# Second attention of a four-layer transformer piece: a new order of the work on TensorE, VectorE and GpSimd, and a key bias added on GpSimd

## Chip, cores, metric

The kernel is one launch on one core of a Trainium2 chip. The metric is the device time of an execution in microseconds (us), as the median of several runs. A core has TensorE (PE in the rows: matmuls, and PEld, its weight loads), VectorE (DVE), ScalarE (ACT), GpSimd (POOL) and SyncE (SP, which only issues transfers here). Each runs its own instructions in the order written; semaphores tie the engines together.

## What is computed

16 sequences of 128 tokens of width 128 pass four layers, each with a residual: a cross attention on a context of 120 rows, a mixture of 8 experts with 2 picked per token, a second cross attention, and a second mixture of experts. The change is in the hand-over from the second layer to the third, and in the third:

```python
x = x + _L0_ffn_ref(_layernorm(x), ...)          # rows sorted by expert, each row of x gets two results back
xn = _layernorm(x)                               # third layer, 8 heads of 128:
q = einsum('bld,hed->bhle', xn, Wq) + bq;  k, v = the same of the context with Wk, bk and Wv, bv
attn = softmax(windowed(q @ k.T));  out = attn @ v
x = x + out.reshape(...) @ Wc.T + bc
```

The windows of the third layer count positions by head (dilations 1, 1, 2, 2, 4, 4, 8, 8), and positions past the end of the context fold onto its last row; a mask `window` of logarithms of counts, added to the scores, does both. Where a window reaches past the context's 120 rows, the key is that of the last row, so the scores need no more than the 120 columns. The key bias adds the same number to all scores of a query and head: `xn . uvec + ubias`.

## The kernel before

**Phases.** Phase a projects for the first layer, phase b is the first attention, then 46 tiles of 128 rows sorted by expert go through the experts (functions with `ct_`), then phase d is the second attention, and phase e the last layer. Every phase is a software pipeline written out by hand: each engine has a list of (lag, stage), and in step k it runs each stage on sequence k - lag, in the order of the list. The lists' order is the order of the engine's instructions, and nothing reorders them. In phase d the pipeline has 16 + 7 steps.

**Phase d, one sequence b.** PE forms the queries of all 8 heads at once from the kept, transposed activations `xT` (`d_queries`, L1716, 8 heads, 16 passes) and VectorE adds `cvec` to make `q2` (`d_queries` on VectorE, L1352). PE multiplies with the context (`d_scores`, L1725), VectorE adds the mask into `s1` (L1361, two pieces), takes the maximum (L1368) and two small differences (L1373, L1376). ScalarE takes the exponentials, one head at a time with its sum (`d_softmax`, L727, 8 pairs). VectorE divides (`d_weights`, L1381 and L1384). The values come from the context, which GpSimd splits in a rounded part `c_hi` and a rest `c_lo` (`d_stage`, L916, L918); PE multiplies both with the value and output weights (`d_values`, L1736, 6 passes) and ScalarE copies the result from PSUM (`d_vw_copy`, L720). PE turns the weights (`d_turn`, L1449, 8 of them, into the same two PSUM banks), ScalarE copies them (`d_aT_copy`, L733), and PE makes the output (`d_output`, L1757). VectorE adds it to `x` (L1390). A tail follows for the last layer: statistics (L1110, L1120), a power on GpSimd (L823, L825), the normalised rows (L1133), a turn on PE (`tail_turn`, L1449), a copy on ScalarE (`tail_evict`, L676), the router's logits on PE (`tail_logits`, L1595), and a split in two parts on GpSimd (`tail_keep`, L835, L837).

**The second half of the hand-over (`c`).** The 16 sequences are in two parts of 7 and 9. The hand-over of a sequence is: two gathers by GpSimd of the experts' rows (`gather`, L900), two weighted additions on VectorE (`c_combine`, L1329, L1333), statistics, power, normalised rows (`c_norm`, L1133), turn, copy (`tail_evict("c")`), `xT` kept by GpSimd (L840), and the key bias: `tail_logits("c")` multiplies with `uvec` (L1595) and adds `ubias` by a second product with a row of ones (L1597), and ScalarE copies the sum to `u1s` (`tail_scores`, L684). Part one's hand-over runs beside the expert tiles, that of part two inside phase d: `d_step(b, late)` gives in step b the sequence 7 + b - 1 - late. So steps 1 to 12 of phase d have hand-over work in them, and the later ones have none.

In the list of PE for phase d `c_turn` stands last in a step, and the next step starts with `d_scores`. On VectorE the hand-over stands last in a step. On GpSimd it stands first (gather, power, keep), then `d_stage`. In `tail_logits("c")` a wait of the second part asks that ScalarE has copied the turned rows of the *next* sequence too (`ev`, b + 2), because both use one PSUM bank.

## Time and profile before

| | |
|---|---|
| median of 3 runs | 568.66 us (568.36 to 569.81) |
| the profiled execution | 569.37 us, of which 567.1 us are the span of the trace |
| PE busy | 478.5 us, 84% of the span |
| VectorE | 370.5 us, 65% |
| ScalarE | 272.1 us, 48% |
| GpSimd | 179.3 us, 32% |
| mean granted clock of PE | 0.942 of full speed |

The page sums the busy time over phases with different limits, so 84% says little of phase d, which takes the stretch from 338 to about 508 us. There the timeline by instruction and the table by stretch are read. Times in rows are us from the start of the span. A row with "x16" is 16 instructions merged, with the time from the first start to the last end; a bracket gives the idle time before it and what ended it. A granted clock of 1.00 is 2.4 GHz, and PE at half of it runs at 1.2 GHz.

### The profile page before, as it was taken

The numbers are of one execution on the slowest core, as the hardware profiler recorded it, in microseconds if no ns is written. First come the engines' busy times: TensorE is split into PE (matmuls) and PEld (weight loads), VectorE is DVE, ScalarE is ACT, GpSimd is POOL, SyncE is SP. The second block draws the span as 40 slices with busy tenths as digits, with TensorE's granted clock in tenths as the row PEclk, the third lists the DMA queues.
The fourth block names the chain that finished last, engine by engine and source line by source line (L and its number), as shares of the span: only waits on it lengthen the run. The fifth ranks groups of instructions, "written<-read, shape, count | busy, mean of one in ns | idle before, by whom it ended". The sixth has DMA issues, their size and how long they took to land.

```text
span 567.1 us, 12474 instructions
## 1 busy us (share of the span) xinstructions
PE 478.5 (84%) x3538; PEld 346.0 (61%) x3538; DVE 370.5 (65%) x1322; ACT 272.1 (48%) x882; POOL 179.3 (32%) x363
## 2 busy tenths in 40 slices
PE   2899999899899795198899996698888999775996
PEld 1444444296466563055566766587778899663785
DVE  5389999886488857055446736757776687627543
ACT  0598898854455442133333332634645566622311
POOL 4223222210044327534636504235353223321000
PEclk9999999999799978589999998879999999995999
DMA  6974536000000000123233310000000000000001
GB/s 124 328 248 138 164 120 175 5 1 16 17 4 5 4 3 29 50 62 103 86 86 95 94 47 29 9 10 16 14 10 3 1 1 2 2 0 1 20 18 38
DMA packets 54526, 30.89 MB, mean 54 GB/s; under 512 B 10172, under 2 KB 52038, under 8 KB 54470
## 3 DMA queue, kind: packets, MB, share of 16 engines
q1 hardware_dynamic: 49766, 24.82, 15.2%
q0 software_dynamic: 2048, 4.20, 2.4%
q10 hardware_dynamic: 2656, 1.18, 0.8%
q8 instruction: 29, 0.48, 0.3%
q14 instruction: 27, 0.22, 0.1%
HBM read 14.45 MB, written 15.73 MB: 53 GB/s over the span
## 4 chain that ended last, share of the span: by engine, by line
PE 37%; DVE 9%; issue 7%; POOL 3%; ACT 2%; DMA 1%; SPq 0%; DVEq 0%; POOLq 0%; ACTq 0%
PE psum L1678 7%; PE psum L1449 5%; PE psum L1716 5%; PE psum L1736 4%; PE psum L1725 4%; PE psum L1695 3%; PE psum L1757 3%; PE psum L1800 3%; PE psum L1787 1%; POOL by_expert L861 1%; PE psum L1777 1%; DVE work L1352 1%; PE psum L1798 1%; DMA by_expert<-scored,rows_at 1%; DMA c_area<-by_expert 1%
## 5 line engine op out<-in xcount | busy, mean ns | idle before, releaser
L625 ACT ACTIVATE wa<-psum,negmax 128x120 f32<-128x120 f32 x256 | 67.9, 376 | 10.3 <-DVE negmax L988 10.3
L1495 PE MATMUL psum<-wa 32*128 32x480 f32 x128 | 63.0, 1082 | 2.1 <-ACT wa L625 2.0
L1449 PE MATMUL psum<-cst,c_area 128*128 128x128 f32 x154 | 35.6, 287 | 31.4 <-DVE c_area L1133 14.0
L1449 PEld LDWEIGHTS psum<-cst,c_area 128*128 128x128 f32 x154 | 21.5, 142 | 60.2 <-issue 23.0
L727 ACT ACTIVATE work<-work,d 128x120 f32<-128x120 f32 x128 | 48.7, 384 | 14.2 <-DVE d L1376 14.2
L693 ACT ACTIVATE c_area<-psum 128x256 f32<-128x256 f32 x46 | 17.7, 384 | 73.8 <-PE psum L1678 73.8
L1678 PE MATMUL psum<-upT,c_area 128*128 x92 | 50.8, 635 | 0.1
L1000 DVE BATCH_NORM_STATS2 scored<-wa 128x120 f32 (+1 forms) x256 | 50.4, 270 | 0.7 <-issue 0.7
L658 ACT ACTIVATE work<-psum 120x1024 f32<-120x1024 f32 x32 | 31.0, 1021 | 35.3 <-PE psum L1612 35.3
L988 DVE TENSOR_REDUCE negmax<-psum 128x8 f32<-128x960 f32 x32 | 36.8, 1150 | 12.5 <-PE psum L1495 12.5
L1315 DVE TENSOR_TENSOR c_area<-psum,c_area 128x256 f32<-128x256 f32 x46 | 19.4, 423 | 38.0 <-ACT c_area L693 38.0
L861 POOL DMA_INDIRECT by_expert<-scored,rows_at x32 | 31.3, 978 | 29.6 <-PE psum L1449 24.3
L900 POOL DMA_INDIRECT c_area<-by_expert,rows_at x32 | 31.3, 979 | 26.2 <-DMA by_expert<-c_area 18.6
L1725 PE MATMUL psum<-ctxT,work 128*128 128x120 f32 x256 | 35.3, 296 | 3.6 <-DVE work L1352 3.6
L799 POOL TENSOR_TENSOR wa<-kT,cst 128x480 f32<-128x480 f32 x16 | 15.8, 986 | 66.1 <-ACT kT L605 66.1
L1725 PEld LDWEIGHTS psum<-ctxT,work 128*128 128x128 f32 x256 | 33.1, 209 | 3.9 <-DVE work L1352 3.9
L1716 PEld LDWEIGHTS psum<-xT,qk 128*128 128x128 f32 x256 | 31.8, 197 | 1.4
L1352 DVE TENSOR_TENSOR work<-psum,cvec 128x1024 f32<-128x1024 f32 x16 | 19.6, 1224 | 19.2 <-PE psum L1716 19.2
L1361 DVE TENSOR_TENSOR work<-psum,cst 128x480 f32<-128x480 f32 x32 | 19.6, 653 | 19.1 <-PE psum L1725 19.1
L1716 PE MATMUL psum<-xT,qk 128*128 128x128 f32 x256 | 31.9, 279 | 0.0
L1757 PE MATMUL psum<-work 120*128 120x128 f32 x256 | 31.3, 275 | 0.4 <-ACT xnT L676 0.4
L1757 PEld LDWEIGHTS psum<-work 120*128 120x128 f32 x256 | 29.8, 192 | 0.6 <-issue 0.6
(279 smaller groups left out, 1117.5 us busy)
## 6 DMA issues: line engine op xcount, KB each, us to landing
by_expert<-work SPq DMA_DIRECT2D x12, 768.0 KB, 4.4
c_area<-by_expert SPq DMA_DIRECT2D x46, 64.0 KB, 1.8
by_expert<-c_area SPq DMA_DIRECT2D x46, 64.0 KB, 1.6
x<-in_x_dram ACTq DMA_DIRECT2D x4, 256.0 KB, 5.4
work<-in_L_ffn_w_down_dram SPq DMA_DIRECT2D x1, 1024.0 KB
wa<-mscratch SPq DMA_DIRECT2D x64, 2.0 KB
out_dram<-wa SPq DMA_DIRECT2D x4, 256.0 KB, 2.3
wa<-in_ctx_dram SPq DMA_DIRECT2D x16, 60.0 KB, 1.9
```

Of the source, the lines that this page charges most:

```text
L625: e = nc.scalar.activation(prob[:, z, hh, :], psum[:, 3 + 2 * half + h // 4, (h % 4) * LK:(h % 4 + 1) * LK], ACT.Exp, bias=negmax[:, z, hh ...
L727: e = nc.scalar.activation(e1[:, z, h, :], s1[:, z, h, :], ACT.Exp, bias=d8[:, z, 3, h:h + 1], accum_out=d8[:, z, 4, h:h + 1])
L861: nc.gpsimd.indirect_dma_start(by_expert[:, :], bass.IndirectOffsetOnAxis(rows_at[:, h, i:i + 1], 0), xrow[:, b, :], None).then_inc(scatte ...
L900: nc.gpsimd.indirect_dma_start(y_rows[:, r, j, :], None, by_expert[:, :], bass.IndirectOffsetOnAxis(rows_at[:, h, i:i + 1], 0)).then_inc(l ...
L988: nc.vector.tensor_reduce(negmax[:, z, half * HALF0:(half + 1) * HALF0].rearrange("p (a h) -> p a h", a=2), psum[:, 3 + 2 * half:5 + 2 * h ...
L1000: s = nc.vector.bn_stats(bnout[:, bass.ds(b * H0 + h, 1), :].rearrange("p a s -> p (a s)"), prob[:, z, h, :])
L1449: return nc.tensor.transpose(dst, src, ident[0:k, 0:k])
L1495: m = nc.tensor.matmul(psum[:, 3 + g, 0:4 * LK], qs[rows, z, :], kexp[rows, z].rearrange("p i k -> p (i k)"), start=True, stop=True)
L1678: nc.tensor.matmul(psum[:, n % 2, :], ct_xT[:, n % 2, :], w, start=True, stop=True).then_inc(ct_up, 1)
L1716: m = nc.tensor.matmul(psum[:, h // 4, (h % 4) * LQ:(h % 4 + 1) * LQ], qk1[:, h, :], xT[:, b, :], start=True, stop=True)
L1725: m = nc.tensor.matmul(psum[:, 2 + h // 4, (h % 4) * LK:(h % 4 + 1) * LK], q2[:, z, h, :], ctxT[:, b, :], start=True, stop=True)
L1757: m = nc.tensor.matmul(dst, a1T[:, z, h, :], vw[:, z, h, :], start=(h == 0), stop=(h == H1 - 1))
```

## The change

Six edits, all in the two places above. (1) On PE `d_queries` moves ahead of the tail turn and `d_values`. (2) On PE `d_output` moves ahead of `d_turn`. (3) On GpSimd `d_stage`, the split of the context, moves to the head of a step; its two instructions now count on one semaphore, `d_cs`. (4) On VectorE the whole hand-over (normalised rows, then combining and statistics of the next sequence) moves from the end of a step to its head, behind `tail_norm("d")`. (5) The product with `ubias` is gone from PE, in the tile phase and in phase d, 16 in all. (6) GpSimd adds `ubias` to `u1s`: seven additions before phase d, and one a step inside it; VectorE waits for that count, `d_ub`, instead of ScalarE's `d_u`.

```diff
+            def c_key_bias(b):
+                pool.wait_ge(d_u, b + 1)
+                nc.gpsimd.tensor_tensor(u1s[:, b, :], u1s[:, b, :], ubias[:, :], ALU.add).then_inc(d_ub, 1)
+
             for k in range(PARTS[0].seqs + 3):
+                c_gather(k, 0)
                 c_tail(k, 0)
+            for b in range(PARTS[0].seqs):
+                c_key_bias(b)
...
-            software_pipeline(pool, [(0, lambda b, z: c_tail(b, 1)), (2, d_stage), (4, tail_rstd("d")),
-                                     (7, tail_keep("d"))], peel=NB)
+            def d_key_bias(b, z):
+                c = d_step(b, 3)
+                if c is not None:
+                    c_key_bias(c)
+
+            software_pipeline(pool, [(2, d_stage), (0, lambda b, z: c_gather(b, 1)), (0, lambda b, z: c_tail(b, 1)),
+                                     (4, tail_rstd("d")), (0, d_key_bias), (7, tail_keep("d"))], peel=NB)
...
-                dve.wait_ge(d_u, b + 1)
+                dve.wait_ge(d_ub, b + 1)
...
-            software_pipeline(dve, [(6, tail_norm("d")), (1, d_scores), (0, d_queries), (2, d_weights),
-                                    (2, add_bias(1, d_xb)), (4, d_residual), (4, tail_stats("d", d_x)), (4, tail_aggr("d")),
-                                    (0, lambda b, z: c_tail(lambda late: d_step(b, late), 1))], peel=NB)
+            software_pipeline(dve, [(6, tail_norm("d")), (0, lambda b, z: c_tail(lambda late: d_step(b, late), 1)),
+                                    (1, d_scores), (0, d_queries), (2, d_weights),
+                                    (2, add_bias(1, d_xb)), (4, d_residual), (4, tail_stats("d", d_x)), (4, tail_aggr("d"))],
+                              peel=NB)
...
-                    m = nc.tensor.matmul(scored_at(ph, b), of["xnT"][:, z, :], weights, start=True, stop=ph != "c")
-                    if ph == "c":
-                        m = nc.tensor.matmul(scored_at(ph, b), ones[0:1, :], ubias[0:1, :], start=False, stop=True)
-                    m.then_inc(s["lg"], 1)
+                    nc.tensor.matmul(scored_at(ph, b), of["xnT"][:, z, :], weights, start=True, stop=True
+                                     ).then_inc(s["lg"], 1)
...
-            software_pipeline(pe, [(1, d_scores), (0, lambda b, z: c_part(c_logits, d_step(b, 3))), (7, tail_turn("d")),
-                                   (3, d_values), (0, d_queries), (3, d_turn), (4, d_output),
+            software_pipeline(pe, [(1, d_scores), (0, lambda b, z: c_part(c_logits, d_step(b, 3))), (0, d_queries),
+                                   (7, tail_turn("d")), (3, d_values), (4, d_output), (3, d_turn),
                                    (7, tail_logits("d", router1)), (0, lambda b, z: c_part(c_turn, d_step(b, 1)))],
                               peel=NB)
```

The next rows are PE's instructions of one full step of phase d before the change (a step in the middle, with all stages in it; six value products stand between the turn and the queries, of which one is shown).

```order
L1725 MATMUL psum<-ctxT,work 128x120 x8
L1595 MATMUL psum<-uvec,work 128x8
L1597 MATMUL psum<-ubias,ones 128x8
L1449 MATMUL psum<-cst,xn 128x128
L1736 MATMUL psum<-vo_hi,c_hi 120x512
...
L1716 MATMUL psum<-xT,qk 128x128 x8
L1449 MATMUL psum<-cst,work 120x128 x8
L1757 MATMUL psum<-work 128x128 x8
L1595 MATMUL psum<-router,xnT 128x8
L1449 MATMUL psum<-cst,c_area 128x128
```

The same step after the change, on PE (line numbers have shifted by 13 to 15):

```order
L1738 MATMUL psum<-ctxT,work 128x120 x8
L1610 MATMUL psum<-uvec,work 128x8
L1729 MATMUL psum<-xT,qk 128x128 x8
L1464 MATMUL psum<-cst,xn 128x128
L1749 MATMUL psum<-vo_hi,c_hi 120x512
...
L1770 MATMUL psum<-work 128x128 x8
L1464 MATMUL psum<-cst,work 120x128 x8
L1610 MATMUL psum<-router,xnT 128x8
L1464 MATMUL psum<-cst,c_area 128x128
```

The queries moved from behind the values to ahead of them, the outputs from behind the turned weights to ahead of them, and the product with `ubias` is gone.

On VectorE the start of phase d before the change (the first row is the addition to the queries of sequence 0, the last the combining of sequence 7, the first of part two; `ew_t` are the expert weights):

```order
L1352 TENSOR_TENSOR work<-psum,cvec 128x1024
L1361 TENSOR_TENSOR work<-psum,cst 128x480 x2
L1368 TENSOR_REDUCE d<-work 128x8
L1373 TENSOR_TENSOR d<-small,d 128x8
L1376 TENSOR_TENSOR d<-small,d 128x8
L1352 TENSOR_TENSOR work<-psum,cvec 128x1024
L1230 TENSOR_SCALAR ew_t<-ew_t 128x9
L1232 RECIPROCAL ew_t<-ew_t 128x9
L1234 TENSOR_TENSOR ew_t<-ew_t 128x9
L1329 SCALAR_TENSOR_TENSOR x<-c_area,ew_t,x 128x128
```

And after it:

```order
L1366 TENSOR_TENSOR work<-psum,cvec 128x1024
L1244 TENSOR_SCALAR ew_t<-ew_t 128x9
L1246 RECIPROCAL ew_t<-ew_t 128x9
L1248 TENSOR_TENSOR ew_t<-ew_t 128x9
L1343 SCALAR_TENSOR_TENSOR x<-c_area,ew_t,x 128x128
L1347 SCALAR_TENSOR_TENSOR x<-c_area,ew_t,x 128x128
L981 MEMSET carried 128x1
L1124 BN_STATS work<-x 128x6
L981 MEMSET carried 128x1
L1134 BN_AGGR work<-work 128x2
L1375 TENSOR_TENSOR work<-psum,cst 128x480 x2
```

The combining of sequence 7, which reads what GpSimd gathers (`c_area`), now stands ahead of the scores of sequence 0 and the queries of sequence 1.

On GpSimd a full step in the middle of phase d before the change (gathers, power, keep, the split of the context, power of the last layer's tail, its keep):

```order
L900 DMA c_area<-by_expert,rows_at 128x128 x2
L823 TENSOR_TENSOR work<-work,eps 128x1
L825 TENSOR_TENSOR work<-work,eps 128x1
L840 COPY xT<-work 128x128
L916 CAST c_hi<-ctxT 128x120
L918 TENSOR_TENSOR c_lo<-ctxT,c_hi 128x120
L823 TENSOR_TENSOR rstd<-mv,eps 128x1
L825 TENSOR_TENSOR rstd<-rstd,eps 128x1
L835 CAST x_hi<-xnT 128x128
L837 TENSOR_TENSOR x_lo<-xnT,x_hi 128x128
```

The same step after the change:

```order
L925 CAST c_hi<-ctxT 128x120
L927 TENSOR_TENSOR c_lo<-ctxT,c_hi 128x120
L900 DMA c_area<-by_expert,rows_at 128x128 x2
L823 TENSOR_TENSOR work<-work,eps 128x1
L825 TENSOR_TENSOR work<-work,eps 128x1
L840 COPY xT<-work 128x128
L823 TENSOR_TENSOR rstd<-mv,eps 128x1
L825 TENSOR_TENSOR rstd<-rstd,eps 128x1
L915 TENSOR_TENSOR small<-small,ubias 128x8
L835 CAST x_hi<-xnT 128x128
L837 TENSOR_TENSOR x_lo<-xnT,x_hi 128x128
```

The split went from behind the powers that wait for VectorE to ahead of the gathers, and the addition of `ubias` is new.

## Rows read from the trace of the kernel before

**Rows 1.** Table by stretch: us, busy us of each engine, granted clock, DMA.

```profile
310.00:334.00 24.00, 24.00 (x135) 17.04 (x134) 14.86 (x64) 9.20 (x36) 10.61 (x21) 1.00 0.27 76
359.00:380.40 21.40, 18.02 (x106) 16.43 (x105) 13.30 (x32) 10.31 (x38) 6.68 (x12) 0.78 0.04 13
380.40:443.02 62.62, 53.50 (x415) 49.80 (x415) 45.92 (x132) 33.30 (x124) 25.49 (x61) 1.00 0.03 10
443.02:483.90 40.88, 40.88 (x334) 39.29 (x334) 30.68 (x70) 25.95 (x97) 10.58 (x30) 1.00 0.01 1
```

**Rows 2.** Timeline of PE, one step of phase d with hand-over: start, us, instruction.

```profile
402.98 0.29 PE L1595 MATMUL psum<-uvec,work 128*128 128x8 f32 x2
403.20 0.38 PE L1597 MATMUL psum<-ubias,ones 1*128 1x8 f32 x2
403.51 0.33 PE L1449 MATMUL psum<-cst,xn 128*128 128x128 f32 x1
404.14 0.50 PE L1736 MATMUL psum<-vo_hi,c_hi 128*120 128x512 f32 x1 [0.30 <-POOL c_lo L918]
...
405.64 1.95 PE L1716 MATMUL psum<-xT,qk 128*128 128x128 f32 x16
407.42 1.04 PE L1449 MATMUL psum<-cst,work 128*120 128x128 f32 x8
...
411.43 0.33 PE L1449 MATMUL psum<-cst,c_area 128*128 128x128 f32 x1 [1.06 <-DVE c_area L1133]
411.59 1.95 PE L1725 MATMUL psum<-ctxT,work 128*128 128x120 f32 x16
```

**Rows 3.** Timeline of VectorE in that step.

```profile
407.62 1.23 DVE L1352 TENSOR_TENSOR work<-psum,cvec 128x1024 f32<-128x1024 f32 x1 [1.63 <-PE psum L1716]
...
411.04 0.33 DVE L1133 TENSOR_SCALAR c_area<-x,work 128x128 f32<-128x128 f32 x1
```

**Rows 4.** Timeline of ScalarE in that step.

```profile
405.84 1.01 ACT L720 COPY work<-psum 120x1024 f32<-120x1024 f32 x1 [1.69 <-PE psum L1736]
...
406.75 0.40 ACT L727 ACTIVATE work<-work,d 128x120 f32<-128x120 f32 x1
...
409.78 0.99 ACT L733 COPY work<-psum 120x1024 f32<-120x1024 f32 x1
...
411.79 0.27 ACT L676 COPY work<-psum 128x128 f32<-128x128 f32 x1 [1.01 <-PE psum L1449]
```

**Rows 5.** Timeline of PE, scores of sequences 11 and 12, without hand-over turn.

```profile
451.50 2.02 PE L1725 MATMUL psum<-ctxT,work 128*128 128x120 f32 x16
...
460.05 2.02 PE L1725 MATMUL psum<-ctxT,work 128*128 128x120 f32 x16
```

**Rows 6.** Timeline of all engines at the start of phase d.

```profile
343.64 1.96 PE L1716 MATMUL psum<-xT,qk 128*128 128x128 f32 x16
...
343.84 1.22 DVE L1361 TENSOR_TENSOR work<-psum,cst 128x480 f32<-128x480 f32 x2 [2.14 <-PE psum L1725]
343.85 0.94 POOL L900 DMA_INDIRECT c_area<-by_expert,rows_at  x1 [0.31 <-issue]
...
347.84 3.67 PE L1725 MATMUL psum<-ctxT,work 128*128 128x120 f32 x16 [2.25 <-DVE work L1352]
...
367.51 2.79 PE L1725 MATMUL psum<-ctxT,work 128*128 128x120 f32 x16
```

**Rows 7.** Use of line 900 (the gathers): from issue to landing.

```profile
DMA to landing us min/median/max: 2.4/2.5/3.0
```

**Rows 8.** Timeline of PE in the drain of phase d.

```profile
483.90 2.02 PE L1725 MATMUL psum<-ctxT,work 128*128 128x120 f32 x16
...
492.99 0.46 PE L1736 MATMUL psum<-vo_hi,c_hi 128*120 128x512 f32 x1 [0.74 <-ACT work L733]
...
506.12 2.02 PE L1757 MATMUL psum<-work 120*128 120x128 f32 x16 [0.45 <-ACT xnT L676]
```

**Rows 9.** Use of line 918 (split of the context on GpSimd): ns min/median/max.

```profile
L918 POOL TENSOR_TENSOR c_lo<-ctxT,c_hi x16: 437/440/450, 359.7 to 494.9; 128x120 fp32r<-128x120 f32 x16
```

More of the change, by code:

```diff
@@ L387, in build @@
         b_xb, d_xb = sem("b_xb"), sem("d_xb")
-        d_u, d_chi, rounded, halved = sem("d_u"), sem("d_chi"), sem("rounded"), sem("halved")
+        d_u, d_ub, rounded, halved = sem("d_u"), sem("d_ub"), sem("rounded"), sem("halved")
         e_gt, e_gts, e_h, e_g, e_gm, e_gps, e_hg, e_y, e_acc = (
@@ L901, in gather, with c_gather, c_tail @@
                                                  bass.IndirectOffsetOnAxis(rows_at[:, h, i:i + 1], 0)).then_inc(ld_y[r], 16)
-            def c_tail(at, h):
+            def c_gather(at, h):
                 if at in range(PARTS[h].seqs):
                     gather(PARTS[h].first + at)
+            def c_tail(at, h):
                 for late, stage in ((1, tail_rstd), (3, tail_keep)):
@@ L909, in c_tail @@
                         stage("c")(b, b % 2)
+            def c_key_bias(b):
+                pool.wait_ge(d_u, b + 1)
+                nc.gpsimd.tensor_tensor(u1s[:, b, :], u1s[:, b, :], ubias[:, :], ALU.add).then_inc(d_ub, 1)
             for k in range(PARTS[0].seqs + 3):
+                c_gather(k, 0)
                 c_tail(k, 0)
+            for b in range(PARTS[0].seqs):
+                c_key_bias(b)
             def d_stage(b, z):
                 reused(pool, d_vwp, b)
-                nc.gpsimd.tensor_copy(c_hi[:, z, :], ctxT[:, b, :]).then_inc(d_chi, 1)
-                pool.wait_ge(d_chi, b + 1)
+                nc.gpsimd.tensor_copy(c_hi[:, z, :], ctxT[:, b, :]).then_inc(d_cs, 1)
+                pool.wait_ge(d_cs, 2 * b + 1)
                 nc.gpsimd.tensor_tensor(c_lo[:, z, :], ctxT[:, b, :], c_hi[:, z, :].bitcast(F32), ALU.subtract
                                         ).then_inc(d_cs, 1)
-            software_pipeline(pool, [(0, lambda b, z: c_tail(b, 1)), (2, d_stage), (4, tail_rstd("d")),
-                                     (7, tail_keep("d"))], peel=NB)
+            def d_key_bias(b, z):
[4 more added lines that the diff above has]
+                                     (4, tail_rstd("d")), (0, d_key_bias), (7, tail_keep("d"))], peel=NB)
         @block.vector
@@ L1729, in d_values @@
             def d_values(b, z):
-                pe.wait_ge(d_cs, b + 1)
+                pe.wait_ge(d_cs, 2 * b + 2)
                 if not isinstance(b, int) or b >= 1:
```

## Prediction

> **What bounds it now.** I read the table by stretch first [rows 1], because the page's 84% for PE is a mean over phases. Between 310 and 334 us, in the expert tiles, PE is busy 24.00 of 24.00 us. Between 443.02 and 483.90, in phase d once the hand-over's turns are over, it is again busy all the time (40.88 of 40.88). Between 380.40 and 443.02, six steps with full hand-over, it is busy only 53.50 of 62.62. A step there takes 62.62/6 = 10.44 us, against 8.55 us in the step from 451.50 to 460.05 [rows 5]. So something holds PE for 1.4 to 1.9 us in each of these steps.
>
> The timeline of one step shows what [rows 2 to 4]. PE's last instruction of the step, the turn of the hand-over, starts after 1.06 us of idleness, released by VectorE's normalised rows (L1133). That instruction stands at the end of VectorE's step, 411.04 - 407.62 = 3.42 us behind the addition to the queries (L1352), which itself had waited 1.63 us for PE's queries (L1716). And PE reached the queries late, since the values ahead of them had waited (0.30 us, 404.14) for GpSimd's `c_lo`. This is a ring: queries on PE, 3.75 us on VectorE (407.62 to 411.37), turn, scores, values, queries. The change opens it in both places.
>
> **Part by part.**
>
> *Product with `ubias` removed.* It holds PE from 403.20 to 403.51, 0.31 us [rows 2]. Seven of the 16 are in the tile phase, where PE is never idle: 7 x 0.31 = 2.2 us, all gained. The other nine are counted in the steps below.
>
> *PE's own work in a full step, afterwards.* The full step from 451.50 to 460.05 takes 8.55 us [rows 5] and has no hand-over turn. Less 0.31, plus 0.16 for the turn (411.43 to 411.59 in rows 2), it is 8.40 us. That is the least a step can take.
>
> *What is late next: ScalarE.* Its order within a step does not change: copy of the hand-over's turn, copy of scores, copy of the tail's turn, values, eight exponentials, turned weights. Moving the queries ahead delays the values on PE by 1.78 us, and the exponentials stand behind the copy of the values. The hand-over's product with `uvec` at the head of PE's next step waits for ScalarE to have copied the next sequence's turn (the condition "b + 2"), and that copy stands behind the turned weights. So there is a new ring. On PE: product with `uvec` to queries 0.24 (0.22 between 402.98 and 403.20, and a little), queries 1.78 (405.64 to 407.42), tail turn 0.1, first value product to ScalarE's copy 1.70 (404.14 to 405.84), together 3.82 [rows 2, 4]. On ScalarE: copy of values to first exponential 0.91, exponentials 3.03 (406.75 to 409.78), turned weights 0.95 (between the 0.91 from the values' copy to its successor and its own length, 0.99), copy of the turn 0.27, then some 0.05 to PE: 5.2 [rows 4]. The sum is 9.0 us, above PE's 8.40. So I take 9.0 us for a step, with PE now waiting some 0.6 us at the product with `uvec`. It holds for steps 4 to 11, in which this wait has a copy of the same step to wait for.
>
> *Can VectorE hold it?* It is busy 45.92/6 = 7.65 us a step [rows 1]; its ring with PE is open now, since the normalised rows come at the head of a step and PE needs them at its end. *GpSimd?* Busy 25.49/6 = 4.25 us. Its `c_lo` is made a whole step before its use, so the 0.30 us goes. The new addition (128x8, two inputs) is not in this trace. It costs at least nothing and at most what 128x120 takes, 0.44 us [rows 9]; I take 0.2, nearer the small end. It is hidden: nobody needs the sum before VectorE's scores one step later, and GpSimd idles over 4 us a step. What is queued behind it are the tail's keep, the split and the gathers. GpSimd gets past a step when VectorE has made that step's last statistics; the combining that reads the next gathers stands at the head of the step after the next, so one whole step of 9.0 and two small instructions, 9.4 us, later. The way through GpSimd is at most all its work, 4.25 + 0.44, about 1 us of gaps, and the slowest landing, 3.0 us [rows 7]: 8.7. It fits, by 0.7 us. The seven additions before phase d fall where GpSimd waits for the last tiles to be stored. If that cover were gone they would cost 7 x 0.2 = 1.4 us.
>
> The Trainium skill, "SBUF — State Buffer", section "Who interferes with whom", says that a VectorE instruction with two inputs in SBUF and a GpSimd instruction that reads SBUF block one another for the whole instruction. By it the new addition could hold VectorE 0.2 to 0.44 us a step. No row here shows such a blocking (line 918 spans 437 to 450 ns over 16 uses), and VectorE would keep about 1 us of slack a step, so by rule or by row the sum is the same.
>
> *Start of phase d: a loss.* VectorE's step 1 now begins with combining sequence 7, which must wait for gathers that start only when the last tiles are stored. The second one is issued at 343.85 [rows 6], ends 0.94 later, and lands 2.5 us from its issue at the earliest (346.4), from its end at the latest (347.3) [rows 7]. I take 347.0. Combining and statistics take 1.3 us, so the scores' addition, at 343.84 before, starts at 348.3. From it PE's second scores follow in 4.0 us (343.84 to 347.84): 352.3 for 347.84, a loss of 4.5 us. It does not last. The next steps were held before by the late normalised rows, and no longer are. At half speed, as at 347.84, the second scores take 3.7 us: 356.0. VectorE's 4.0 follow: 360.0. Then PE's scores, queries and values up to ScalarE's copy, 1.9 + 1.8 + 1.7: 365.4; the copy, 1.0; the turned weights and the hand-over's turn, 1.1: scores of sequence 3 at about 367.6, against 367.51. Loss and gain cancel there.
>
> *Step 4 and PE's clock.* The scores at 367.51 take 2.79 us for 1.95, and the granted clock is 0.78 over 359 to 380.4 [rows 1, 6]: half speed (1.2 GHz) for a good part of it, after PE had idled. Afterwards, in step 4, ScalarE's exponentials begin at 366.3 (values copied) and take 3.0, then 0.95 and 0.27: the `uvec` product at 370.5. Behind it PE has its 8.24 us less the scores' 1.85, nearly 6.4: step 4 ends at 376.8, against 380.40: -3.6 us at full clock. The low clock cost this step some 2.5 us before (12.89 for 10.44). In the new order PE idles longer early on, from 345.6 (343.64 + 1.96, rows 6) to 352.3, and less later. So 0 to 4 us of it come off the gain, and I take 2.
>
> *Steps 5 to 11.* Step 4's `uvec` product at 370.5, that of step 11 seven rings later at 433.6, scores of sequence 11 another 6.4 us on, at 440.0. So this stretch takes 440.0 - 376.8 = 63.2 us. Before it took 451.50 - 380.40 = 71.1: -7.9 us. *Step 12*: PE-bound, -0.3 us. *Steps 13 to 15*: PE-bound at 7.95 us ((483.90 - 460.05)/3) [rows 5, 8], no change.
>
> *Drain.* From the last scores to the last output were 22.2 us (483.90 to 506.12) [rows 8]. The values of sequence 14, at 492.99, wait for ScalarE's copy of turned weights, which stands behind the exponentials; that stays. But then the output of the earlier sequence fills the 1 us in which the values are copied, and the turn follows at once: -1 us for each of two steps, together 20.2 us: -2.0 us.
>
> **Sum.** -2.2 (tiles) + 0 (start) - 3.6 (step 4) - 7.9 - 0.3 - 2.0 = -16.0, and 2.0 back for the clock: -14.0 us. The profiled execution took 569.37 us, so 555.4 by it; it was 0.7 above the median of the runs, 568.66, and I forecast by the median: **554.6 us**. Its own range is 552 to 557, by the clock's 0 to 4 us and some 0.5 for landing.
>
> **Rivals.**
> - *ScalarE does not bind; PE runs unbroken.* For it: ScalarE is busy only 33.30/6 = 5.6 us a step. Against: the ring is of waits, not of work. A step takes 8.40: seven times 0.6 is 4.2 us more: 550.4 us. Chance 0.12.
> - *The start costs more.* VectorE stands in front of the gather, PE idles 6.8 us and later again; its clock stays at 1.2 GHz through two more steps. For it: 0.78 in rows 1 with less idleness at the start. A step with low clock lost 2.5 us before: 2.5 to 5 us more, 557 to 560 us. Chance 0.20.
> - *The ring is not opened by the order*: another wait keeps steps at 10.4 us. Against: rows 2 name the releaser each time. Left are tiles, step 12 and drain: -4.5, 564 us. Chance 0.07.
> - *Slower: each step's combining waits for the gather.* VectorE's whole step, and with it queries and scores, now stands behind it. The ring through GpSimd spans two steps: 8.7 us on GpSimd and landing, and some 7.7 us of VectorE's work. It binds once it passes 2 x 9.0, and to eat 14 us over seven steps it must reach 2 x 11.0 = 22 us, so a landing of over 8 us, against 3.0 at most in rows 7. Then 570 us and more. Chance 0.04.
>
> Chances: main case 0.57, the rivals 0.12, 0.20, 0.07, 0.04. The range is 550 to 560.5 us: it holds the main case, PE unbroken, and most of the clock's. A change under 0.3% (1.7 us) can't be told from none in this kernel. Faster: 0.94; within 0.3%: 0.02; slower: 0.04.
>
> **What will show it.** Period of PE's scores in steps 5 to 11: 9.0 (right), 8.4 (rival one), over 10 (three or four). In front of the `uvec` product PE idles 0.5 to 0.7 us, released by ScalarE's L676; the idle times before the hand-over's turn and the first values are gone. VectorE's first combining shows a wait for the gather of 4 to 5 us, and PE's second scores start 8.7 us after its second queries, not 4.2 (343.64 to 347.84). From last scores to last output: 20 us. PE busy throughout the tiles at the same clock, with 2.2 us less. The prediction is wrong if the granted clock is below 1 beyond the start of phase d, or if the combining waits in the middle.

## Result, and the profile after

The changed kernel takes **555.85 us** (median of 4 runs, 554.14 to 558.48). The kernel before, run beside it, takes 569.23 us (4 runs, 568.36 to 571.15). The ratio is 0.9756, 95% interval 0.9721 to 0.9791. The forecast was 554.6 us, in a range of 550 to 560.5. The profiled execution has a span of 554.8 us, against 567.1: 12.3 us less, where the medians differ by 13.4.

The table by stretch of the changed kernel: a stretch of the tiles, the two parts of the start of phase d, seven steps with hand-over (scores of sequence 4 to scores of 11), the last full steps, and the drain. Columns as in [rows 1].

```profile
310.00:334.00 24.00, 22.46 (x123) 14.90 (x122) 15.38 (x68) 8.69 (x34) 11.18 (x22) 1.00 0.30 82
343.40:352.70 9.30, 3.83 (x32) 3.64 (x32) 5.32 (x16) 1.13 (x6) 6.54 (x10) 0.89 0.15 37
352.70:368.00 15.30, 12.48 (x81) 11.64 (x82) 12.37 (x31) 7.48 (x37) 6.45 (x13) 0.84 0.05 13
377.29:440.30 63.01, 58.62 (x472) 55.47 (x470) 51.57 (x142) 38.21 (x146) 27.78 (x68) 1.00 0.04 10
448.50:472.40 23.90, 23.90 (x199) 22.99 (x197) 18.51 (x44) 15.62 (x58) 6.51 (x19) 1.00 0.01 2
472.40:492.80 20.40, 15.90 (x120) 14.32 (x118) 9.47 (x33) 11.96 (x35) 7.81 (x20) 1.00 0.00 1
```

A step with hand-over takes 63.01/7 = 9.00 us, where it took 10.44. PE still idles 63.01 - 58.62 = 4.39 us over these seven steps. In the tiles PE is no longer busy all the time: 22.46 of 24.00 us. The work was taken out, and the stretch didn't get shorter (E5 measures it).

PE's timeline in one step of the changed kernel (answers to [rows 2]):

```profile
406.84 0.36 PE L1610 MATMUL psum<-uvec,work 128*128 128x8 f32 x2 [0.55 <-ACT work L676]
407.06 2.03 PE L1729 MATMUL psum<-xT,qk 128*128 128x128 f32 x16
...
408.95 0.48 PE L1749 MATMUL psum<-vo_hi,c_hi 128*120 128x512 f32 x1
...
410.43 1.95 PE L1770 MATMUL psum<-work 120*128 120x128 f32 x16
...
413.23 0.31 PE L1464 MATMUL psum<-cst,c_area 128*128 128x128 f32 x1
413.37 1.94 PE L1738 MATMUL psum<-ctxT,work 128*128 128x120 f32 x16
415.87 0.36 PE L1610 MATMUL psum<-uvec,work 128*128 128x8 f32 x2 [0.56 <-ACT work L676]
```

The waits at the first value product and at the hand-over's turn are gone. One is left, 0.55 us, where it was expected: at the product with `uvec`, until ScalarE's copy of a turn (L676). ScalarE's timeline in the same step (answers to [rows 4]) shows how that copy becomes late:

```profile
406.44 0.26 ACT L676 COPY work<-psum 128x128 f32<-128x128 f32 x1
...
410.63 1.01 ACT L720 COPY work<-psum 120x1024 f32<-120x1024 f32 x1 [1.13 <-PE psum L1749]
411.54 0.40 ACT L727 ACTIVATE work<-work,d 128x120 f32<-128x120 f32 x1
...
414.57 1.00 ACT L733 COPY work<-psum 120x1024 f32<-120x1024 f32 x1
...
415.46 0.27 ACT L676 COPY work<-psum 128x128 f32<-128x128 f32 x1
```

From the copy of the values on, at 410.63, ScalarE is busy without a gap up to the turn's copy at 415.46: 4.83 us to its start. The last instruction of the chain ends at 415.73, and PE's product starts at 415.87.

The start of phase d, all engines (answers to [rows 6]):

```profile
344.28 0.94 POOL L900 DMA_INDIRECT c_area<-by_expert,rows_at  x1 [0.31 <-issue]
345.27 1.96 PE L1729 MATMUL psum<-xT,qk 128*128 128x128 f32 x16
347.55 0.35 DVE L1343 SCALAR_TENSOR_TENSOR x<-c_area,ew_t,x 128x128 f32<-128x128 f32 x1 [3.69 <-DMA c_area<-by_expert,rows_at]
348.76 1.19 DVE L1375 TENSOR_TENSOR work<-psum,cst 128x480 f32<-128x480 f32 x2
352.73 3.77 PE L1738 MATMUL psum<-ctxT,work 128*128 128x120 f32 x16 [5.50 <-DVE work L1366]
360.54 2.05 PE L1738 MATMUL psum<-ctxT,work 128*128 128x120 f32 x16 [1.59 <-DVE work L1366]
```

VectorE waits 3.69 us at the head of its step for the gather, and the scores' addition, ready since 345.44 (343.39 + 2.05, the end of PE's first scores), starts at 348.76. PE idles 5.50 us and then needs 3.77 us for scores of 1.96 us. By the third scores (360.54) it is at full speed again.

Use of line 915, the new addition on GpSimd (ns min/median/max):

```profile
L915 POOL TENSOR_TENSOR small<-small,ubias x16: 190/200/315, 334.7 to 449.5; 128x8 f32<-128x8 f32 x16
```

The addition costs the 0.2 us that it was priced at, or 0.3 in some steps (last section). The gathers take 2.5 to 3.5 us from issue to landing, median 2.6, and only the first combining waits for one.

Where the 12.3 us between the two spans come from, stretch by stretch, with the terms of the forecast:

| stretch | before | after | difference | forecast |
|---|---|---|---|---|
| up to the first queries of phase d | 338.49 | 340.12 | +1.6 | -2.2 |
| first queries to scores of sequence 3 | 29.02 | 27.84 | -1.2 | 0 |
| step 4 (with the clock's charge) | 12.89 | 9.33 | -3.6 | -1.6 |
| scores of 4 to scores of 11 | 71.10 | 63.01 | -8.1 | -7.9 |
| step 12 | 8.55 | 8.19 | -0.4 | -0.3 |
| steps 13 to 15 | 23.85 | 23.89 | 0 | 0 |
| drain: scores of 15 to its output | 22.22 | 20.36 | -1.9 | -2.0 |
| to the end | 60.98 | 62.06 | +1.1 | 0 |

Step 4 in the table by stretch: the kernel before, E5 (which has the orders of before), and the changed kernel:

```profile
367.51:380.40 12.89, 11.71 (x69) 10.83 (x68) 7.42 (x22) 5.37 (x20) 3.65 (x7) 0.74 0.04 11
373.28:384.30 11.02, 9.84 (x66) 9.14 (x66) 7.42 (x22) 5.37 (x20) 3.65 (x7) 0.85 0.06 13
367.96:377.29 9.33, 8.20 (x67) 7.74 (x66) 8.17 (x24) 5.67 (x23) 2.27 (x4) 1.00 0.05 16
```

PE idles 1.18, 1.18 and 1.13 us in it. What differs is its busy time, and with it the granted clock.

### The profile page after: what moved, and what is told of

Its sections match the earlier page's. It is cut to its first block, busy times and chain, and to the rows that moved or that the text cites. A ratio compares the mean times of both kernels' runs of the same rounds, so it can differ in the third digit from the quotient of the medians.

```text
span 554.8 us, 12426 instructions
## 1 busy us (share of the span) xinstructions
PE 471.0 (85%) x3506; PEld 338.8 (61%) x3506; DVE 370.3 (67%) x1322; ACT 270.1 (49%) x882; POOL 183.5 (33%) x379
## 3 DMA queue, kind: packets, MB, share of 16 engines
q10 hardware_dynamic: 2656, 1.18, 0.8%
## 4 chain that ended last, share of the span: by engine, by line
PE 32%; ACT 9%; DVE 7%; issue 6%; DMA 3%; POOL 2%; SPq 1%; DVEq 0%; POOLq 0%; ACTq 0%
PE psum L1691 6%; ACT work L727 6%; PE psum L1729 4%; PE psum L1749 4%; PE psum L1464 4%; PE psum L1813 3%; PE psum L1738 2%; PE psum L1770 2%; PE psum L1708 2%; ACT work L733 2%; DMA c_area<-by_expert 1%; PE psum L1800 1%; PE psum L1790 1%; POOL by_expert L861 1%; PE psum L1610 1%
## 5 line engine op out<-in xcount | busy, mean ns | idle before, releaser
L625 ACT ACTIVATE wa<-psum,negmax 128x120 f32<-128x120 f32 x256 | 67.8, 376 | 10.5 <-DVE negmax L1002 10.4
L1464 PEld LDWEIGHTS psum<-cst,c_area 128*128 128x128 f32 x154 | 22.7, 149 | 47.7 <-issue 26.4
L1738 PE MATMUL psum<-ctxT,work 128*128 128x120 f32 x256 | 33.5, 287 | 8.4 <-DVE work L1366 8.4
L1738 PEld LDWEIGHTS psum<-ctxT,work 128*128 128x128 f32 x256 | 31.6, 201 | 9.0 <-DVE work L1366 9.0
L1770 PEld LDWEIGHTS psum<-work 120*128 120x128 f32 x256 | 31.0, 192 | 2.7 <-ACT work L733 1.2
L1729 PEld LDWEIGHTS psum<-xT,qk 128*128 128x128 f32 x256 | 30.6, 196 | 0.0
L720 ACT COPY work<-psum 120x1024 f32<-120x1024 f32 x16 | 16.2, 1012 | 27.6 <-PE psum L1749 27.6
```

The costliest lines, as they stand in the source:

```text
L625: e = nc.scalar.activation(prob[:, z, hh, :], psum[:, 3 + 2 * half + h // 4, (h % 4) * LK:(h % 4 + 1) * LK], ACT.Exp, bias=negmax[:, z, hh ...
L1464: return nc.tensor.transpose(dst, src, ident[0:k, 0:k])
L1729: m = nc.tensor.matmul(psum[:, h // 4, (h % 4) * LQ:(h % 4 + 1) * LQ], qk1[:, h, :], xT[:, b, :], start=True, stop=True)
L1738: m = nc.tensor.matmul(psum[:, 2 + h // 4, (h % 4) * LK:(h % 4 + 1) * LK], q2[:, z, h, :], ctxT[:, b, :], start=True, stop=True)
L1770: m = nc.tensor.matmul(dst, a1T[:, z, h, :], vw[:, z, h, :], start=(h == 0), stop=(h == H1 - 1))
```

## Experiments

They ran in three groups, each beside the kernel before. That one took 577.51 us beside E1 to E4 and 576.95 beside E5 to E8, both on one chip, and 570.17 beside E9 to E12, on another. So ratios to it are compared, and stretches of the traces.

### E1: the product with `uvec` behind the queries

```diff
-software_pipeline(pe, [(1, d_scores), (0, ...c_logits...), (0, d_queries),
+software_pipeline(pe, [(1, d_scores), (0, d_queries), (0, ...c_logits...),
```

> The changed kernel with one stage moved on PE: the product with uvec stands behind the queries of the next sequence, not ahead of them. Theory (ring through ScalarE): the 1.78 us of queries leave the ring, which falls from 8.97 to about 7.2 us, below PE's own 8.4 us. So the scores of steps 5 to 11 come every 8.4 us, PE is unbroken there, and seven steps save 0.55 us each: some 3.9 us less than the changed kernel, about 551 to 552 us. Rival (PE is held at the product by something other than the order, such as VectorE's step or GpSimd's keep of xT): the period stays at 9.0 us and the idle time only moves to another instruction; no difference in time.

Measured: 552.91 us, ratio 0.9595 (0.9559 to 0.9631). Scores of 4 to 11, by the table by stretch:

```profile
379.26:436.00 56.74, 56.74 (x471) 54.67 (x470) 50.54 (x144) 38.22 (x146) 27.85 (x68) 1.00 0.04 11
```

PE is busy 56.74 of 56.74 us: 8.1 us a step, 6.3 less than in the changed kernel, and step 4 takes 7.95 instead of 9.33. The product stands at 406.93 without a wait, between the queries and the tail turn:

```profile
406.93 0.29 PE L1610 MATMUL psum<-uvec,work 128*128 128x8 f32 x2
...
407.13 0.48 PE L1749 MATMUL psum<-vo_hi,c_hi 128*120 128x512 f32 x1
```

So ScalarE's ring was what held the step. It gave back more than expected: PE's own work in a step is 7.95 us in step 4 and in the first two of the seven, which have no tail, 8.2 in the next four and 8.05 in the last, not the 8.40 of the forecast, and step 4 gains too.

### E2: edit 1 undone (queries behind the values again)

```diff
-(0, d_queries), (7, tail_turn("d")), (3, d_values), (4, d_output), (3, d_turn),
+(7, tail_turn("d")), (3, d_values), (0, d_queries), (4, d_output), (3, d_turn),
```

> The changed kernel with edit 1 alone undone: on PE the tail turn and the values stand ahead of the queries again. Theory (ring through ScalarE): edit 1 made this ring, by putting 1.78 us of queries in front of the values. Without it the ring is 7.2 us, the step is PE's 8.4 us, and the kernel gains some 3 to 4 us over the changed one, since the outputs still cover ScalarE's copy of the values. Rival (the queries ahead of the values are what opened the old ring): the period goes back up to 9.5 to 10.4 us and the kernel loses 4 to 10 us.

Measured: 556.75 us, 0.9647 (0.9627 to 0.9668). Steps of 57.05/7 = 8.15 us; step 4 takes 9.42 (9.33 in the changed kernel). The kernel is faster without this edit (6.8 us below E4's kernel, which runs as the changed one does): edit 1 put 1.78 us of queries between the product and the values, and so made the new ring longer than PE's work (9.0 - 1.8 = 7.2 us without them).

### E3: edit 2 undone (turned weights ahead of the output again)

```diff
-(3, d_values), (4, d_output), (3, d_turn),
+(3, d_values), (3, d_turn), (4, d_output),
```

> The changed kernel with edit 2 alone undone: turned weights ahead of outputs again, so behind the values nothing covers ScalarE's copy of them. Theory: PE waits about 1.3 us for that copy in every step that has values, the period of steps 5 to 11 is 9.7 us and of steps 13 to 15 9.3 for 7.95, and the drain loses its 1.9 us again: +12 to +14 us, so about as long as the kernel before. Rival (edit 2 acts in the drain alone): +2 us.

Measured: 573.72 us, 0.9929 (0.9909 to 0.995). Steps of 66.60/7 = 9.51 us, and 9.33 in steps 13 to 15, which have no hand-over. PE's timeline names the wait:

```profile
418.28 0.40 PE L1749 MATMUL psum<-vo_hi,c_lo 128*120 128x512 f32 x1
419.87 1.06 PE L1464 MATMUL psum<-cst,work 128*120 128x128 f32 x8 [1.19 <-ACT work L720]
```

Values and turned weights share two PSUM banks. When the turn follows at once, PE waits 1.19 us until ScalarE has copied the values; the queries had covered this before, and the output covers it now. Without edit 2 the change is worth only 3.8 us: the kernel takes 10.2 us more than E4's, where 12 to 14 were expected. This says what edit 2 is worth once edit 1 has moved the queries away from between values and turn. What it is worth alone no run shows.

### E4: edit 3 undone (the split of the context behind the hand-over on GpSimd)

```diff
-software_pipeline(pool, [(2, d_stage), (0, ...c_gather...), (0, ...c_tail...),
+software_pipeline(pool, [(0, ...c_gather...), (0, ...c_tail...), (2, d_stage),
```

> The changed kernel with edit 3 alone undone: GpSimd splits the context behind gathers, powers and keep again. Theory: the split was late before because the power ahead of it waited for statistics at the end of VectorE's step; with the statistics at the head of VectorE's step it is in time in either place: no difference, PE's values start without a wait. Rival (the place of the split gave the 0.3 us a step): PE waits 0.3 us before the values in steps 4 to 12, but hidden under the ring through ScalarE or +2 to +3 us.

Measured: 563.52 us, 0.9754 (0.9738 to 0.977), steps of 62.99/7 = 9.00 us. No difference: the other edits already bring the hand-over's powers early enough.

### E5: edits 5 and 6 alone, on the orders of before

The stage lists have the order of the kernel before; only `ubias` goes to GpSimd.

> The kernel before with edits 5 and 6 alone: product with ubias gone from PE, added by GpSimd; all orders as before. Theory (in the tile phase PE's turn of the next tile waits for VectorE, and the product with ubias was hidden in that wait; in phase d the wait for c_lo and for the hand-over hides it but for steps 11 and 12): the tiles keep their period of 4.22 us per two, and the gain is 0.6 to 1 us, too little to tell. Rival (PE bound in the tiles, as predicted): period 3.9 us per two tiles, and 2.2 us more gain, 2.8 us in all.

Measured: 575.03 us, 0.9977 (0.9954 to 0.9999). A pair of tiles takes 4.22 us with and without the product. In the changed kernel, PE's timeline in the tiles:

```profile
319.04 0.29 PE L1610 MATMUL psum<-uvec,work 128*128 128x8 f32 x2
...
319.76 0.30 PE L1464 MATMUL psum<-cst,c_area 128*128 128x128 f32 x1 [0.27 <-DVE c_area L1323]
...
323.25 0.29 PE L1610 MATMUL psum<-uvec,work 128*128 128x8 f32 x2
```

and VectorE's:

```profile
321.57 0.42 DVE L1329 TENSOR_TENSOR c_area<-psum,c_area 128x256 f32<-128x256 f32 x1 [1.18 <-ACT c_area L693]
...
322.11 0.34 DVE L1147 TENSOR_SCALAR c_area<-x,work 128x128 f32<-128x128 f32 x1
...
323.56 0.27 DVE L1323 COPY c_area<-psum 128x128 f32<-128x128 f32 x1
```

PE finishes the turn of the tile's rows and waits for VectorE's copy of them (L1323), which stands behind the whole hand-over of a sequence (normalised rows, combining, statistics). VectorE itself begins that stretch late, 1.18 us idle until ScalarE has worked on what PE's product with `upT` gave. So the period is that of a ring through three engines: PE's turn (319.76) and product (320.00), ScalarE, VectorE from 321.57 to its copy at 323.56, and PE's turn again (323.98), 4.22 us later. The product with `ubias` had lain in PE's wait, and that is why PE had looked fully busy.

### E6: in the tiles, the normalised rows one tile earlier

```diff
-(0, lambda n: c_tail(lambda late: c_step(n, late), 2))])
+(0, lambda n: c_tail(lambda late: c_step(n, late), 1))])
```

> The changed kernel with the normalised rows of the hand-over's first part on VectorE one tile earlier, so that VectorE's hand-over is spread over both tiles of a pair. Theory (VectorE's copy of the turned tile behind the hand-over sets the tiles' period of 4.22 us): with 0.25 us less in the loaded tile PE's wait of 0.27 us before the second turn goes and the period falls to about 3.95 us for seven pairs: -1.5 to -1.9 us. Rival (the tiles' period is set by loads of tiles or by ScalarE): 4.22 us stays, no difference.

Measured: 562.14 us, 0.9742 (0.9711 to 0.9773). From the first product with `uvec` to the seventh it takes 24.07 us (316.74 to 340.81) against 25.09 in E4's trace (317.04 to 342.13): 1.0 us less, where 1.5 to 1.9 were expected. In the total it can't be told.

### E7: the first hand-over of phase d last in its step on VectorE, the others first

```diff
+def d_hand_over(first):
+    def run(b, z):
+        if (b == 1) == first:
+            c_tail(lambda late: d_step(b, late), 1)
+    return run
...
-software_pipeline(dve, [(6, tail_norm("d")), (0, ...c_tail...), (1, d_scores), ...
+software_pipeline(dve, [(6, tail_norm("d")), (0, d_hand_over(False)), (1, d_scores), ...
+                        (0, d_hand_over(True))], peel=NB)
```

> The changed kernel, but VectorE's hand-over of step 1 (combining of sequence 7, which waits for the gather) at the end of the step as before; in all later steps at the head. Theory (head of line): the scores' addition of sequence 0 no longer stands behind the gather, PE's second scores start 4.2 us after its second queries instead of 7.5, and since later steps are not held by late normalised rows the gain carries through: -3 to -4.5 us against the changed kernel. Rival (the chain recovers by itself, or PE's low clock takes it): scores of sequence 3 at the same distance from the first queries, 27.8 us, and no difference.

Measured: 563.97 us, 0.9777 (0.9753 to 0.9802). The second scores come 9.35 us after the first queries instead of 12.6, and yet the fourth ones come only 1.2 us earlier (26.66, changed kernel 27.84). In the total it can't be told from E4's 0.9754. My theory that the 3 us would last fell. VectorE and PE in this kernel:

```profile
356.31 2.04 PE L1744 MATMUL psum<-ctxT,work 128*128 128x120 f32 x16 [2.24 <-DVE work L1366]
359.08 0.35 DVE L1147 TENSOR_SCALAR c_area<-x,work 128x128 f32<-128x128 f32 x1 [0.96 <-POOL work L825]
360.60 1.19 DVE L1375 TENSOR_TENSOR work<-psum,cst 128x480 f32<-128x480 f32 x2
364.57 1.77 PE L1744 MATMUL psum<-ctxT,work 128*128 128x120 f32 x9 [4.31 <-DVE work L1366]
```

The hand-over of sequence 7 now ends step 1 and that of sequence 8 begins step 2, one right behind the other, with a wait of 0.96 us for GpSimd's power between them. The scores done at 358.3 are added at 360.60, and PE idles 4.31 us ahead of its third scores. The wait moved by one step.

### E8: edit 4 undone (hand-over last in VectorE's step)

```diff
-software_pipeline(dve, [(6, tail_norm("d")), (0, ...c_tail...), (1, d_scores), (0, d_queries), ...
+software_pipeline(dve, [(6, tail_norm("d")), (1, d_scores), (0, d_queries), ..., (0, ...c_tail...)], ...
```

> The changed kernel with edit 4 alone undone: on VectorE the hand-over stands last in all steps of phase d. Theory (two rings of nearly the same length): queries, VectorE 3.75 us, turn, scores, and VectorE's scores 2.85 us again give a ring of 8.8 to 8.9 us, just under the ring through ScalarE, 8.97, so the steps stay at 9.0 us; and the start has no head-of-line wait, so the kernel is 2 to 4 us faster than the changed one. Rival (edit 4 opened the old ring, as the prediction had it): the period is above 9.5 us and the kernel loses 4 us or more.

Measured: 562.72 us, 0.9762 (0.9738 to 0.9786). Steps of 62.41/7 = 8.92 us. The second scores come at 9.35, the fourth at 27.20, and step 4 takes 9.86: of the 3.3 us of the start 0.6 are left, and step 4 gives 0.5 back. No difference in the total, where a gain of 2 to 4 us was expected. With the queries early, normalised rows at the end of VectorE's step are early enough.

### E9: the product late (E1) and the normalised rows earlier in the tiles (E6)

> The product with uvec stands behind the queries in phase d, and in the tiles the normalised rows are made one tile earlier. Theory: the gains add up, since the two edits are in different phases: steps of 8.1 us (56.7 us from scores of sequence 4 to those of 11) as with the product moved alone, and 4.0 us instead of 4.22 for each pair of tiles, which took 1.0 us off six pairs: 551.9 us where the product moved alone takes 552.9, a ratio near 0.958 to the kernel before. Rival: the last tiles are held by transfers or by the experts' weights, so that phase d starts no earlier: 0.9595. The stretch of the tiles shows it; the total may not, since the two lie within 0.2% of each other.

Measured: **548.4 us**, 0.9614 (0.9592 to 0.9637), against 550.9 us, 0.9656 (0.9629 to 0.9683), for E1's kernel in the same group (E11) and 556.55, 0.9769 (0.9742 to 0.9796), for the changed kernel (E12). It is faster than both kernels of the case. Beside E1's kernel the intervals touch. In the tiles (315 to 335 us) PE waits for L1323 once, and the products shown are 3.96 us apart; from the first product to the seventh it takes 24.35 us (311.40 to 335.75) against E11's 25.24:

```profile
319.86 0.29 PE L1610 MATMUL psum<-uvec,work 128*128 128x8 f32 x2
320.00 0.63 PE L1464 MATMUL psum<-cst,c_area 128*128 128x128 f32 x2
...
323.82 0.29 PE L1610 MATMUL psum<-uvec,work 128*128 128x8 f32 x2
```

### E10: the product late, and behind values and queries (edit 1 undone as well)

```diff
+software_pipeline(pe, [(1, d_scores), (7, tail_turn("d")), (3, d_values), (0, d_queries),
+                       (0, ...c_logits...), (4, d_output), (3, d_turn),
```

> The product with uvec stands late and the queries stand behind the values again, as in the kernel before (edit 1 undone, product moved). Theory: edit 1 is not needed. Nothing but the product's wait tied the values to ScalarE's last copy, and behind the values and queries it comes late enough: its ring then spans two steps, (3.4 + 1.9 + 0.1 + 1.7) us on PE and 5.2 us on ScalarE, 12.3 us for two steps of 8.1, so it binds nothing. Steps of 8.1 us (57 us from scores of 4 to those of 11) and step 4 at 8 us, as with the product moved alone: ratio 0.9595. Rival: with the queries late VectorE's addition comes late, as in the kernel before, and the next scores wait for it: steps of 8.5 to 9 us, 3 to 6 us more, ratio 0.965 to 0.970.

Measured: 556.48 us, 0.9759 (0.9728 to 0.979). Steps of 62.40/7 = 8.91 us: both the theory and the rival's reason are wrong. PE, first in a step without a tail, then in one with it:

```profile
388.03 0.47 PE L1749 MATMUL psum<-vo_hi,c_hi 128*120 128x512 f32 x1 [0.53 <-ACT work L733]
...
408.86 0.29 PE L1610 MATMUL psum<-uvec,work 128*128 128x8 f32 x2
409.67 2.02 PE L1770 MATMUL psum<-work 120*128 120x128 f32 x16 [0.52 <-ACT xnT L676]
```

ScalarE:

```profile
409.19 0.17 ACT L684 COPY small<-psum 128x8 f32<-128x8 f32 x1 [3.56 <-PE psum L1610]
409.25 0.27 ACT L676 COPY xnT<-psum 128x128 f32<-128x128 f32 x1
409.41 1.03 ACT L720 COPY work<-psum 120x1024 f32<-120x1024 f32 x1
```

I had moved the product on PE and forgotten what is queued behind its reader. On ScalarE the copy of the product (L684) stands ahead of the tail's copy and of the values' copy. The values were ready at 407.3; ScalarE stood 3.56 us at L684, and copied them at 409.41. PE's output, which asks for the tail's copy, waits 0.52 us in each step that has a tail. It starts 0.81 us behind the product, where 0.15 is enough without the wait (382.56 to 382.71): 8.2 + 0.66 is the 8.9. In the first two of the seven steps, which have no tail, the wait stands ahead of the values, for ScalarE's late copy of the turned weights (0.53 us), and they take 8.7 us for 7.95. In E1 the turn and the values lie between the product and the output, and cover the wait for the tail's copy. The nearest comparison is E2, which has the same orders but for the product: 8.15 us a step with it at the head, 8.91 with it behind the queries.

### E11 and E12: E1's kernel and the changed kernel again

> The same kernel as with the product with uvec moved behind the queries alone, to have it beside the others on one chip. Theory: 0.9595 again, steps of 8.1 us. Rival: part of its lead over the changed kernel was the chip's: then the ratio comes within 0.005 of the changed kernel's here.

> The changed kernel unchanged, on the same chip as the experiments. Theory: ratio 0.975 to 0.977, steps of 9.0 us, as the two runs that differ from it by edits without effect gave. Rival: on this chip the change is worth less or more, by over 0.003, and then the comparisons of experiments with its ratio on the first chip are off by as much.

E11: ratio 0.9656, and in its trace 56.75 us for the seven steps. E12: 0.9769, and 63.02 us. The changed kernel's ratio is the same as on the first chip (0.9756) within its interval. That of E1's kernel was 0.006 lower on the other chip, where the kernel before is slower; the two intervals just touch, and the seven steps are the same to 0.01 us. So a comparison within a group holds, and one between groups is good to some 0.006.

## Why the prediction held

**The old ring opened, and ScalarE's took over (right).** The period of 9.0 us was worked out from single durations of the trace before, and 9.00 was measured, with 0.55 us of wait at the product that was named and the releaser that was named. E1 shows the cause: taking the product out of the ring gives 8.1 us. The rival with PE unbroken was wrong for this kernel and right for E1's. The forecast had the change open the old ring in two places. E2 and E8 each undo one of them, and the steps stay at 8.15 and 8.92 us, while E5, with both undone and the other orders of before too, has steps of 10.4. So with the other edits in, either place alone is enough.

**The signs.** No later combining waited for a gather, and the granted clock was 1.00 from 360.54 us to the end of the drain, so neither sign of being wrong came. Two sizes were off: VectorE's first combining waited 3.69 us and not 4 to 5, and the second scores started 7.46 us behind the second queries (352.73 - 345.27) and not 8.7.

**Which edit does it.** Undone alone, edit 2 takes most of the gain with it (0.9929, E3), edit 3 or edit 4 changes nothing that can be told (E4, E8), and edit 1 gives time back: it costs (63.01 - 57.05)/7 = 0.85 us in each of the seven steps. But with the product late, edit 1 is needed (E10). Undoing one edit doesn't price it alone: edit 2 covers a wait that edit 1 lays bare, and edits 1 and 4 open the same ring. The forecast took the change as a whole and had not asked which edit does what.

**Tiles: the term of -2.2 us was wrong, 0 measured (E5).** The step that failed is "PE is never idle" in the tiles. A product of 0.31 us that PE runs while it would otherwise wait for VectorE's copy looks like work in the table. The table said 24.00 of 24.00, and the timeline before had no wait of PE to show. What I could have read is that the ring through PE, ScalarE and VectorE is as long as PE's work.

**Start: mechanism right, size off.** The loss at the second scores was 12.61 - 9.35 = 3.3 us instead of 4.5: the second gather was issued 4.16 us after the first queries (344.28 - 340.12), against 5.36 before (343.85 - 338.49). At the fourth scores 27.84 us stand against 29.02, but E5, with the orders of before, took 27.42, and E12, the changed kernel again, 27.60. So the gain or loss there is within what one order shows from one execution to another, and the forecast of none stands. E7 and E8 show that little is won by avoiding the loss: the next steps take it back.

**Step 4 and the clock: charged 2.0 us, not seen.** The low clock was over by the third scores, and step 4 ran at a granted clock of 1.00. It did so in all twelve traces that have any of the new orders. Before, step 4 took 12.89 us at 0.74. In E5, with the same orders, it took 11.02, at 0.85. So some 1.9 of the 3.6 us come and go with the clock from one execution to another. The other 1.7 can't be put down to the order's waits: PE idles as long in E5's step 4 (1.18 us) as in the changed kernel's (1.13), and is busy 9.84 us against 8.20, still partly at the low clock. The forecast's 9.2 us for this step at full clock (376.8 - 367.6) stands against 9.33; the 2.0 on top were charged for nothing.

**PE's own work in a step: 8.40 in the forecast, 8.2 measured.** It only sized the rival with PE unbroken. The rows show where the 0.2 us went. From the product with `uvec` to the tail's turn it took 0.53 us before (453.37 to 453.90, both products) and 0.14 in E1 (406.93 to 407.07): 0.39 less, not 0.31. And right behind the hand-over's turn the scores take 1.78 us to the next product (403.35 to 405.13 in E1), against 1.87 in the step that the forecast started from (451.50 to 453.37).

**Drain: -2.0 forecast, -1.9 measured.** In the total, two wrong terms, -2.2 (tiles) and +2.0 (clock), cancelled, so 554.6 for 555.85 is closer than its parts deserve; that much was luck. The rest of the difference lies outside the change: +1.6 us up to phase d, where E11 and E12, with the same order up to there, differ by 2.7 (340.44 and 337.77), and +1.1 behind the last output, where E1 and E9, with the same order, take 53.7 and 54.9 us from the last layer's first product to the end.

## What to carry to other kernels

When a stage is moved on one engine, write down for every other engine what stands behind the instruction that reads it, and add up the ring: the new one through ScalarE was found that way, and E10 failed for want of it. An engine that a table shows fully busy may still be part of a ring; taking work from it gave nothing in E5, and the stretch got shorter once the ring did (E6 and E9). Undo the edits of a large change one at a time: here undoing one lost most of the gain, undoing two changed nothing, and undoing one gave 0.85 us a step. But edits that cover for one another need a run with both undone, and that one is missing here.

## What the runs showed of the hardware

The granted clock in the drain differs between executions with the same order of instructions. E12, PE's second group of values after the last scores:

```profile
479.00 0.47 PE L1749 MATMUL psum<-vo_hi,c_hi 128*120 128x512 f32 x1 [2.17 <-ACT work L733]
```

E11, the same instruction:

```profile
473.97 0.63 PE L1749 MATMUL psum<-vo_hi,c_hi 128*120 128x512 f32 x1 [2.17 <-ACT work L733]
```

The idle time ahead of them is the same, 2.17 us. Yet in E11 this value product takes 0.63 us instead of 0.47, the five behind it start 0.43 us apart instead of 0.23, and its drain takes 21.91 us instead of 20.35 (mean granted clock 0.92 and 1.00 over it). Of the traces with outputs ahead of turned weights, those of the first profile, E1, E9 and E12 have the short drain (20.35 to 20.36 us) and E2, E4, E6, E7, E8, E10 and E11 the long one (21.5 to 22.0). E1 and E11 are the same kernel. So 1.6 us of a profiled execution of this kernel are left to that, and a term of this size should be read from several.

GpSimd's new addition takes 0.19 us in five of its steps of phase d and 0.31 or 0.32 in four. In those four it starts inside VectorE's second addition of the combining (two inputs), and ends just behind it. Timeline of VectorE and GpSimd in the changed kernel, at 378, at 387 and at 481 us:

```profile
377.90 0.35 DVE L1347 SCALAR_TENSOR_TENSOR x<-c_area,ew_t,x 128x128 f32<-128x128 f32 x1
378.25 0.19 POOL L915 TENSOR_TENSOR small<-small,ubias 128x8 f32<-128x8 f32 x1
...
387.06 0.35 DVE L1347 SCALAR_TENSOR_TENSOR x<-c_area,ew_t,x 128x128 f32<-128x128 f32 x1
387.17 0.31 POOL L915 TENSOR_TENSOR small<-small,ubias 128x8 f32<-128x8 f32 x1
...
480.85 1.38 DVE L1398 TENSOR_TENSOR work<-work,d 128x960 f32<-128x960 f32 x1
481.15 1.21 POOL L925 CAST c_hi<-ctxT 128x120 fp32r<-128x120 f32 x1
```

VectorE's instruction (L1347) takes 0.35 us either way: GpSimd waits, and VectorE loses nothing that the trace shows. That GpSimd is held up while the other has two inputs at work is what the Trainium skill, "SBUF — State Buffer", section "Who interferes with whom", states, and these rows agree for a VectorE instruction that came first; the cost was 0.12 us, hidden.

The last two rows, from the drain, show more. GpSimd's rounding of the context (L925) takes 0.28 us elsewhere (406.15) and 1.21 here, and ends 0.13 us behind VectorE's division (L1398, two inputs). That division takes 1.16 us elsewhere (410.50) and 1.38 here, where it starts 0.10 us behind the start of a two-input instruction of GpSimd (L837, 480.75, 0.46 us long). So the hold-up is not always 0.1 us, and VectorE can be the one that is slowed.
